# Computing the dt projection of a state-space block with its weights loaded and 512 tokens moved, in a fused three-block kernel

## The chip, the cores and the metric

The kernel is one program on one core of a Trainium2 chip. The metric is the device time of one execution in microseconds (us), the median of several runs. A core has a matrix engine (TensorE, PE in the profile, whose weight loads are listed as PEld), a vector engine (DVE), a scalar engine (ACT), GpSimd (POOL), and DMA queues driven from the SyncE (SP) and POOL instruction streams. Each engine works through its own stream in order; the streams meet at semaphores. A matmul here has a loaded operand (up to 128 columns that stay in the array) and a moved operand (up to 512 columns that stream through it); its result goes to PSUM.

## What is computed

The reference runs three blocks on x (2 sequences of 512 tokens, 1024 features): a Mamba-2 block with an MLP, a quantised product with a context, and a feed-forward block. The change lies in the first block. Cut to what matters:

```
h = rmsnorm(layernorm(x)) * ln1_w
z, xs, Bs, Cs, dt = split(h @ w_in.T)      # widths 1024, 256, 256, 1024, 8
xBC = silu(causal_conv4([xs, Bs, Cs]) + conv_b)
dt  = softplus(dt + dt_bias)               # 8 heads
a   = dt * -exp(A_log)                     # its cumulative sums per chunk of 128 tokens
...                                        # decays, attention within a chunk, states from chunk to chunk
y   = (Y + D * xs) * silu(z);  y @ w_out.T
```

The dt projection is thus a product of the 1024 tokens (2 x 512) with 1024 features by only 8 columns of weights.

## The kernel before

Activations are kept with features on the partitions: `AH` and `AL` are [128, 8, 1024], the high and low part of the normalised input (8 feature tiles, 1024 tokens). A product of single precision is made of three matmuls in the reduced form of fp32: high weights by high activations, high by low, low by high (`three`, line 656 holds the matmul). One block of 128 output features is `block_mm`: 8 feature tiles x 3 x 2 halves of 512 tokens = 48 matmuls with a 128x128 load each.

The work around the change, in the order in which TensorE takes it (block at line 651 and below):

- `first_pair(0)`: the first two convolution blocks, into the PSUM pairs `ps[0]` and `ps[1]`, as the activation tiles come in.
- The dt projection (lines 713 to 719): for each of 8 tiles of 128 tokens and each of 8 feature tiles, the activations are the loaded operand (128x128) and the weights are moved, 16 columns (high and low part of 8 heads, line 716) and then 8 columns (low activations by high weights, line 718). That makes 128 matmuls, whose result has tokens on the partitions, in `ps[2]`.
- `conv_pair(1)` to `conv_pair(5)`: two convolution blocks each, for `ps[0]` and for `ps[1]`. Each block waits for its weights (`s_ready`) and for VectorE to be done with the former block of this PSUM pair (`s_conv`). Between `conv_pair(4)` and `conv_pair(5)` stand two small matmuls for the cumulative sums (lines 726, 727).
- Then two waits, for `s_conv` at 14 (VectorE has finished all 12 convolution blocks) and for `s_csx` at 2, and the state-space stage: 8 chunks of 128 tokens. Each chunk begins with 12 matmuls of a z block into `ps[0]` (`block_mm(ps[0], ..., range(0, 2))`), then come two matmuls of the decay rows into `ps[1]` (line 741), two into `ps[2]` (line 748, which also waits until ScalarE has done all 12 silus), 6 more of z, the transposes (line 754), 6 more of z, line 759, the other 24 of z, and the head products (766, 767, 770).

VectorE follows with its own list. `conv_pair(i)` at line 1557: for each of the two blocks it makes the low part of the weights of a block two further on (`weights_lo`, line 1222, waits for ScalarE's high part), waits until TensorE has summed its block, and applies the four taps (line 1566 and three times line 1568); the last tap signals `s_conv`. Ahead of `conv_pair(0)` VectorE scales the residual input (line 1554, 8 instructions). After `conv_pair(0)` come the dt steps (lines 1579 to 1598): 14 small operations on 128x64 which go back and forth with ScalarE (an exponential, a logarithm, another exponential: lines 1146 to 1149). Then the loop of the other pairs.

ScalarE's list: `conv_silu` (line 1136) makes for each block the high part of the weights (line 920, when TensorE is done with the old weights of this slot), waits for the taps (`s_conv`) and applies silu (line 1141). `conv_silu(0, 0)` stands ahead of the dt functions, the loop of the others behind them.

Weights come by SyncE's queue, two raw slots; block n is loaded (line 389) when the low part of block n - 2 is made. GpSimd stores the scaled residual and copies x in DRAM after line 1554 (lines 594, 595, 4 MB each).

```
for t in range(NC):
    for k in range(KT):
        pe.matmul(ps[2][:, col:col + 2 * HEADS], AH[:, k, tok], wdt_hl[:, k, :, :], ...)
        ins = pe.matmul(ps[2][:, col:col + HEADS], AL[:, k, tok], wdt_hl[:, k, 0, :], ...)
```

Of the kernel before, what the change touches and what calls it, by code (L numbers as in the profile page):

```python
# [8 lines left out]
ACT = mybir.ActivationFunctionType  # L9

P = 128
BATCH, SEQ, DM = 2, 512, 1024
TOK = BATCH * SEQ
KT = DM // P
HEADS, GROUPS = 8, 2
HPG = HEADS // GROUPS
CHUNKS = SEQ // P
NC = BATCH * CHUNKS
TAPS = 4
CONV_TILES = (2 * 256 + DM) // P  # L20
# [124 lines left out]
def build(nc, x_t, ctx, w_mamba, w_dt, w_gu, w_dn, f_gu, f_dn, b_gu, b_dn, params, shapes_only,  # L145
# [9 lines left out]
    AH = at("act_hi", 0, [P, KT, TOK], F32R)  # L155
    AL = at("act_lo", 32 * KB, [P, KT, TOK], F32R)
# [13 lines left out]
    scr_r = at("scratch_r", R0, [P, 8, TOK], F32)  # L170
# [47 lines left out]
    def scr_u(j):  # L218
        return scr_r[:, j, :]

    def scr_c(j):
        return scr_c0[:, j, :] if j < 4 else scr_c1[:, j - 4, :]

# [46 lines left out]
    shp = small("tri_ident_mask", [P, 3, P])  # L270
# [5 lines left out]
    wdt_hl = small("w_dt_hi_lo", [P, KT, 2, HEADS], F32R)  # L276
# [23 lines left out]
    ps = [nc.alloc_psum_tensor(f"pair{i}", [P, TOK], F32) for i in range(4)]  # L300
# [6 lines left out]
    HALF = (slice(0, H), slice(H, TOK))  # L307
# [3 lines left out]
    def sem(name):  # L311
        return nc.alloc_semaphore(name)
# [11 lines left out]
    s_hs, s_hfree = sem("hs_ready"), sem("h_region_free")  # L324
    s_conv, s_silu = sem("conv_summed"), sem("conv_silu")
    s_dtm, s_dte, s_dts, s_csm, s_csx, s_exps = (sem(n) for n in ("dt_summed", "dt_exp_in", "dt_act", "cs_summed", "cs_exp_in", "cs_exp"))
    s_seq = sem("sequence_columns_ready")
    s_stage, s_bx, s_rr = sem("chunk_stage_free"), sem("bx_chunk_ready"), sem("cs_rhs_ready")
    s_yt, s_cs, s_ecs, s_msk, s_dec = sem("y_taken"), sem("cs_rows"), sem("exp_cs"), sem("cs_masked"), sem("decay_ready")
# [321 lines left out]
    def _(pe):  # L651
# [9 lines left out]
        def block_mm(out, wi, ks=range(KT), last_inc=s_used):  # L661

            for k in ks:
                ins = three(out, wi, k, AH[:, k, :], AL[:, k, :], k == 0, k == KT - 1)
            if last_inc is not None:
                ins.then_inc(last_inc, 1)
# [29 lines left out]
        for k in range(KT):  # L696
            pe.wait_ge(s_x[k], 16)
            ins = ones_mm(ps[2], hs[:, k, :], k == 0, k == KT - 1)
# [10 lines left out]
        pe.wait_ge(s_ready, 2)  # L709
        first_pair(0)  # L710

        for t in range(NC):
            col = t * 2 * HEADS
            tok = slice(t * P, (t + 1) * P)
            for k in range(KT):
                pe.matmul(ps[2][:, col:col + 2 * HEADS], AH[:, k, tok], wdt_hl[:, k, :, :],  # L716
                          start=k == 0, stop=False, skip_group_check=True)
                ins = pe.matmul(ps[2][:, col:col + HEADS], AL[:, k, tok], wdt_hl[:, k, 0, :],
                                start=False, stop=k == KT - 1, skip_group_check=True)
        ins.then_inc(s_dtm, 1)  # L720

        with pe.Fori(1, CONV_TILES // 2 - 1) as i:
            conv_pair(i)

        pe.wait_ge(s_csx, 1)
        pe.matmul(ps[2][:, 256:320], tri, a_all[:, :, :], start=True, stop=True)
        pe.matmul(ps[2][:, 320:384], ones[:, :], a_all[:, :, :], start=True, stop=True).then_inc(s_csm, 1)
        conv_pair(CONV_TILES // 2 - 1)
        pe.wait_ge(s_conv, CONV_TILES + 2)
        pe.wait_ge(s_csx, 2)  # L730


        with pe.Fori(0, BATCH) as b:
            for c in range(CHUNKS):
                q = b * CHUNKS + c
                pe.wait_ge(s_ready, q + (N_Z + 1))
                pe.wait_ge(s_z, q + 1)
                block_mm(ps[0], c % 2, range(0, 2), None)
                pe.wait_ge(s_rr, q + 1)
                for g in range(GROUPS):  # L740
                    ins = pe.matmul(ps[1][:, g * 512:(g + 1) * 512], ones[:, :], cs_rhs[:, g * HPG:(g + 1) * HPG, :],  # L741
                                    start=True, stop=False, skip_group_check=True)
                ins.then_inc(s_cs, 1)
                pe.wait_ge(s_bx, q + 1)
                pe.wait_ge(s_silu, CONV_TILES)
                pe.wait_ge(s_yt, q + 1)
                for g in range(GROUPS):
                    pe.matmul(ps[2][:, g * 512:(g + 1) * 512], bx_cur[:, 2 + g, :],  # L748
                              xbc[:, 4 + g * HPG:4 + (g + 1) * HPG, bass.ds(b * SEQ + c * P, P)],
                              start=True, stop=True)  # L750
                block_mm(ps[0], c % 2, range(2, 3), None)
                pe.wait_ge(s_state, b * (CHUNKS + 1) + (c + 1))
                for j in range(4):
                    ins = pe.transpose(ps[3][:, j * P:(j + 1) * P], bx_cur[:, j, :], ident)
                ins.then_inc(s_stage, 1)
                block_mm(ps[0], c % 2, range(3, 4), None)
                pe.wait_ge(s_ecs, q + 1)
                for g in range(GROUPS):
                    ins = pe.matmul(ps[1][:, g * 512:(g + 1) * 512], ident_bf[:, :],
                                    mask_bf[:, :].unsqueeze(1).to_broadcast([P, HPG, P]),  # L760
                                    start=False, stop=True, skip_group_check=True)
                ins.then_inc(s_msk, 1)
                block_mm(ps[0], c % 2, range(4, KT))
                pe.wait_ge(s_att, q + 1)
                for h in range(HEADS):
                    pe.matmul(ps[2][:, h * P:(h + 1) * P], x_dt[:, h, :], att[:, h, :], start=True, stop=False)  # L766
                    ins = pe.matmul(ps[2][:, h * P:(h + 1) * P], state[:, h, :], c_dec[:, h, :], start=False, stop=True)  # L767
                ins.then_inc(s_y, 1)
                for g in range(GROUPS):
                    ins = pe.matmul(ps[3][:, g * 512:(g + 1) * 512], b_tm[:, g, :], x_end[:, g * HPG:(g + 1) * HPG, :],  # L770
                                    start=True, stop=True)
                ins.then_inc(s_st, 1)
# [109 lines left out]
        for k in range(KT):  # L882
            pe.wait_ge(s_q1, k + 1)
            for half in range(2):
                ins = pe.matmul(ps[3][:, half * 512:(half + 1) * 512], ones_bf[:, :], q1[:, k, half * 512:(half + 1) * 512],
                                start=k == 0, stop=k == KT - 1)
            if k == KT - 1:
                ins.then_inc(s_row, 1)
            for o in range(2):
                ins = ctx_mm(o, k)  # L890
# [15 lines left out]
    def _(act):  # L906
# [229 lines left out]
        def conv_silu(i, j0):  # L1136
            for s in range(2):
                weights_hi_at(i, 2, j0 * 2 + s + 2, s)
                act.wait_ge(s_conv, i * 2 + (j0 * 2 + s + 3))
                tile = xbc[:, i * 2 + (j0 * 2 + s), :]  # L1140
                act.activation(tile, tile, ACT.Silu).then_inc(s_silu, 1)

        conv_silu(0, 0)

        act.wait_ge(s_dte, 1)
        act.activation(ncs_all[:, :, :], ncs_all[:, :, :], ACT.Exp).then_inc(s_dts, 1)
        act.wait_ge(s_dte, 2)
        act.activation(gtot_all[:, :, :], a_all[:, :, :], ACT.Ln).then_inc(s_dts, 1)
        act.activation(par[:, PA:PA + HEADS], par[:, PA:PA + HEADS], ACT.Exp).then_inc(s_dts, 1)
        with act.Fori(0, CONV_TILES // 2 - 2) as i:  # L1150
            conv_silu(i, 1)
        act.wait_ge(s_csx, 2)
        act.activation(gtot_all[:, :, :], gtot_all[:, :, :], ACT.Exp).then_inc(s_exps, 1)
        act.activation(dend_all[:, :, :], dend_all[:, :, :], ACT.Exp).then_inc(s_exps, 1)
# [61 lines left out]
    def _(dve):  # L1216
# [355 lines left out]
                ins.then_inc(s_conv, 1)  # L1572

        conv_pair(0)


        dtf = dt_all[:, :, :]
        dve.wait_ge(s_dtm, 1)
        dtp = ps[2][:, 0:NC * 2 * HEADS].rearrange("p (a two b) -> p a two b", a=NC, two=2)
        own.then(TT(dtf, dtp[:, :, 0, :], par[:, PDT:PDT + HEADS].unsqueeze(1).to_broadcast([P, NC, HEADS]), ALU.add))  # L1580
        own.then(TT(dtf, dtp[:, :, 1, :], dtf, ALU.add))
        own.then(STT(ncs_all[:, :, :], dtf, -1.0, dtf, ALU.mult, ALU.max))
# [15 lines left out]
        STT(a_all[:, :, :], dtf, -1.0, par[:, PA:PA + HEADS].unsqueeze(1).to_broadcast([P, NC, HEADS]),  # L1598
            ALU.mult, ALU.mult).then_inc(s_csx, 1)

        with dve.Fori(1, CONV_TILES // 2 - 1) as i:
            own.enter(i - 1, 7)
            conv_pair(i)
            own.leave(CONV_TILES // 2 - 2)


        dve.wait_ge(s_csm, 1)
# [195 lines left out]
```

## Time and profile before

| | us |
|---|---|
| median of 3 runs | 2303.24 (2302.9 to 2304.55) |
| the profiled execution, its own time | 2303.8 |
| its span, first to last instruction | 2302.0 |
| PE busy | 2153.9 (94%) |
| DVE busy | 1778.3 (77%) |
| ACT busy | 1007.7 (44%) |
| mean granted TensorE clock | 0.963 |

How to read it: the engines' busy times overlap each other; "idle before" in a row is the time in which the engine waited ahead of the instruction, with what released it; a granted clock of 1.00 is 2.4 GHz and 0.50 is 1.2 GHz. The durations of pipelined matmuls overlap as well, so what one costs is read from the distance between starts, or from the chain, where a stretch is divided by its count. The stretch that the change touches lies between 54 us and 240 us of the span.

### The profile page before, as it was taken

To read this page: it belongs to the slowest core of one execution; us is meant where nothing else is said; L and a number is where in the kernel's file an instruction comes from. 1 tells how busy PE (TensorE), PEld (TensorE's weight loads), DVE (VectorE), ACT (ScalarE), POOL (GpSimd) and SP (SyncE) were. 2 spreads that over 40 slices of the span, in tenths; PEclk is the share of its full clock that TensorE was granted. 3 is DMA by queue.
4 is the path that set the end of the run, shared out by engine and by line. 5 is a ranking of instruction groups with operands and counts; after the bars stand their busy time and mean duration, and the time that the engine had idled before them with its cause. 6 is when DMAs were issued, how large, how long until landed. Compare 5 with 4: busy or idle time off the path is not lost.

```text
span 2302.0 us, 26720 instructions
## 1 busy us (share of the span) xinstructions
PE 2153.9 (94%) x9346; PEld 1715.3 (75%) x9346; DVE 1778.3 (77%) x2518; ACT 1007.7 (44%) x1596; POOL 118.0 (5%) x195
## 2 busy tenths in 40 slices
PE   6998998978999999999999966689999999999999
PEld 2886776856888888888888822468888888788887
DVE  4755556469777888887978778889898888788785
ACT  3333223325555555554544331555545555444442
POOL 0000110000000000000000000000000000000000
PEclk8799999989999999999999978799999999999999
DMA  3411002524778888889330221156666666674301
GB/s 114 165 46 46 19 28 72 150 39 134 279 274 285 298 299 289 293 300 350 123 134 1 75 82 73 56 177 237 217 226 221 219 226 213 224 279 142 115 19 55
DMA packets 124316, 379.42 MB, mean 165 GB/s; under 512 B 14432, under 2 KB 14560, under 8 KB 120544
## 3 DMA queue, kind: packets, MB, share of 16 engines
q1 hardware_dynamic: 105456, 308.61, 39.1%
q0 software_dynamic: 18736, 69.22, 8.3%
q8 instruction: 70, 1.15, 0.2%
q14 instruction: 54, 0.44, 0.1%
HBM read 312.76 MB, written 69.21 MB: 166 GB/s over the span
## 4 chain that ended last, share of the span: by engine, by line
PE 84%; DVE 10%; DMA 2%; ACT 2%; issue 2%; DVEq 0%; SPq 0%; ACTq 0%
PE pair L823 40%; PE pair L848 23%; PE pair L656 14%; PE pair L684 3%; DVE ring_lo L1326 1%; DVE comb_lo L1376 1%; DMA wd_spill<-down_formed 1%; PE pair L767 1%; PE pair L766 1%; DMA down_formed<-f_dn 1%; PE pair L748 1%; PE pair L741 1%; DMA coeff_in<-b_dn 1%; PE pair L770 1%; PE pair L716 1%
## 5 line engine op out<-in xcount | busy, mean ns | idle before, releaser
L823 PE MATMUL pair<-comb_lo,ring_hi 128*128 128x512 f32 x1568 | 615.2, 392 | 0.0
L848 PE MATMUL pair<-inner_ring_a,ring_hi 128*128 128x512 f32 x1120 | 345.0, 389 | 0.6 <-DVE second_copy_b L1430 0.3
L823 PEld LDWEIGHTS pair<-comb_lo,ring_hi 128*128 128x128 f32 x1568 | 298.1, 190 | 61.2
L823 PE MATMUL pair<-comb_hi,ring_hi 128*128 128x512 f32 x672 | 265.7, 395 | 32.9 <-DVE comb_lo L1376 22.9
L823 PE MATMUL pair<-comb_hi,ring_lo 128*128 128x512 f32 x672 | 264.4, 393 | 0.0
L848 PEld LDWEIGHTS pair<-inner_ring_a,ring_hi 128*128 128x128 f32 x1120 | 210.1, 188 | 44.9 <-issue 1.4
L848 PE MATMUL pair<-inner_ring_a,ring_lo 128*128 128x512 f32 x560 | 217.8, 389 | 0.0
L823 PE MATMUL pair<-comb_hi_b,ring_hi 128*128 128x512 f32 x448 | 176.4, 394 | 15.0 <-ACT first_copy_b L1077 8.2
L823 PE MATMUL pair<-comb_hi_a,ring_hi 128*128 128x512 f32 x448 | 175.7, 392 | 10.8 <-ACT first_copy_a L1077 10.1
L823 PEld LDWEIGHTS pair<-comb_hi,ring_hi 128*128 128x128 f32 x672 | 128.0, 190 | 64.7 <-issue 26.9
L656 PE MATMUL pair<-act_hi,weights_hi 128*128 128x512 f32 x448 | 151.1, 419 | 26.6 <-DVE act_lo L1269 18.7
L823 PE MATMUL pair<-comb_hi_b,ring_lo 128*128 128x512 f32 x448 | 175.7, 392 | 0.0
L823 PE MATMUL pair<-comb_hi_a,ring_lo 128*128 128x512 f32 x448 | 175.0, 391 | 0.0
L998 ACT ACTIVATE ring_hi<-ring_sum 128x512 fp32r<-128x512 f32 x168 | 106.0, 631 | 143.3 <-DVE ring_sum L1313 138.9
L823 PEld LDWEIGHTS pair<-comb_hi,ring_lo 128*128 128x128 f32 x672 | 127.9, 190 | 27.1
L656 PE MATMUL pair<-act_lo,weights_hi 128*128 128x512 f32 x448 | 141.6, 398 | 0.0
L656 PE MATMUL pair<-act_hi,weights_lo 128*128 128x512 f32 x448 | 141.1, 397 | 0.0
L848 PE MATMUL pair<-inner_ring_b,ring_hi 128*128 128x512 f32 x448 | 138.1, 389 | 0.1
L656 PEld LDWEIGHTS pair<-act_hi,weights_hi 128*128 128x128 f32 x448 | 85.5, 194 | 52.7 <-issue 35.8
L848 PEld LDWEIGHTS pair<-inner_ring_a,ring_lo 128*128 128x128 f32 x560 | 105.1, 188 | 21.8
L1096 ACT ACTIVATE pair<-pair 128x1024 f32<-128x1024 f32 x84 | 84.7, 1009 | 72.7 <-DVE pair L1460 72.3
L1326 DVE TENSOR_TENSOR ring_lo<-ring_sum,ring_hi 128x512 fp32r<-128x512 f32 x168 | 115.0, 685 | 0.0
(343 smaller groups left out, 3931.9 us busy)
## 6 DMA issues: line engine op xcount, KB each, us to landing
coeff_in<-f_gu SPq DMA_DIRECT2D x56, 512.0 KB, 5.0
coeff_in<-b_gu SPq DMA_DIRECT2D x56, 512.0 KB, 5.9
base_in<-b_gu SPq DMA_DIRECT2D x56, 512.0 KB, 4.4
weights_raw<-w_mamba SPq DMA_DIRECT2D x28, 512.0 KB, 3.4
raw_a<-w_gu SPq DMA_DIRECT2D x28, 512.0 KB, 6.1
raw_a<-w_gu SPq DMA_DIRECT2D x56, 256.0 KB, 5.6
u_spill<-gate_a POOLq DMA_DIRECT2D x56, 256.0 KB, 5.4
coeff_in<-f_dn SPq DMA_DIRECT2D x28, 512.0 KB, 4.8
```

The costliest lines, as they stand in the source:

```text
L656: ins = pe.matmul(out[:, half * 512:(half + 1) * 512], w[:, wi, wcol * P:(wcol + 1) * P], a[:, half * 512:(half + 1) * 512], start=first a ...
L684: ins = pe.matmul(out[:, half * 512:(half + 1) * 512], ones[:, :], src[:, half * 512:(half + 1) * 512], start=first, stop=last)
L716: pe.matmul(ps[2][:, col:col + 2 * HEADS], AH[:, k, tok], wdt_hl[:, k, :, :], start=k == 0, stop=False, skip_group_check=True)
L741: ins = pe.matmul(ps[1][:, g * 512:(g + 1) * 512], ones[:, :], cs_rhs[:, g * HPG:(g + 1) * HPG, :], start=True, stop=False, skip_group_che ...
L748: pe.matmul(ps[2][:, g * 512:(g + 1) * 512], bx_cur[:, 2 + g, :], xbc[:, 4 + g * HPG:4 + (g + 1) * HPG, bass.ds(b * SEQ + c * P, P)], star ...
L766: pe.matmul(ps[2][:, h * P:(h + 1) * P], x_dt[:, h, :], att[:, h, :], start=True, stop=False)
L767: ins = pe.matmul(ps[2][:, h * P:(h + 1) * P], state[:, h, :], c_dec[:, h, :], start=False, stop=True)
L823: ins = pe.matmul(out, wt[:, slot, col], a, start=t in (0, 1, 3) and kk == 0 and n == 0, stop=kk == KH - 1 and n == 2, skip_group_check=True)
L848: ins = pe.matmul(out, wt[:, slot, col], a, start=t in (0, 1, 3) and k == 0 and n == 0, stop=k == SC_PAIRS - 1 and n == 2, skip_group_chec ...
L998: act.activation(WRH[:, slot, :], src, ACT.Copy).then_inc(s_whi, 1)
L1096: act.activation(dif_ps[:, :], dif_ps[:, :], ACT.Abs, accum_out=coef_all[:, kind, n:n + 1]).then_inc(s_ab, 1)
L1326: TT(WRL[:, slot, :], src, WRH[:, slot, :].bitcast(F32), ALU.subtract).then_inc(s_wlo, 1)
```

## The change

It has three parts. First, the dt projection: the weights (16 or 8 columns) become the loaded operand and 512 tokens are moved, 32 matmuls in place of 128. The result now has the heads on 16 partitions; ScalarE copies it to an SBUF tile of 16 x 1024, TensorE does `conv_pair(1)` meanwhile, and then eight full-fp32 matmuls with that tile as the loaded operand and a 16x16 identity moved turn it back to tokens on partitions, in `ps[3]`. Second, in order to fit, ScalarE takes the copy ahead of `conv_silu(0, 0)` and does `conv_silu(0, 1)` ahead of the dt functions, and VectorE does `conv_pair(1)` ahead of the dt steps. Third, TensorE enters the state-space stage with a wait for `s_conv` at 13 alone; the waits for 14 and for `s_csx` stand behind the first 12 matmuls of z.

```diff
+    dt_rows = scr_r[0:2 * HEADS, 0, :]
...
+    s_dtr, s_dtc = sem("dt_rows_summed"), sem("dt_rows_copied")
...
         first_pair(0)
+        for k in range(KT):
+            for half in HALF:
+                pe.matmul(ps[2][0:2 * HEADS, half], wdt_hl[:, k, :, :], AH[:, k, half],
+                          start=k == 0, stop=False, skip_group_check=True)
+                ins = pe.matmul(ps[2][0:HEADS, half], wdt_hl[:, k, 0, :], AL[:, k, half],
+                                start=False, stop=k == KT - 1, skip_group_check=True)
+        ins.then_inc(s_dtr, 1)
+        conv_pair(1)
+        pe.wait_ge(s_dtc, 1)
         for t in range(NC):
-            col = t * 2 * HEADS
-            tok = slice(t * P, (t + 1) * P)
-            for k in range(KT):
-                pe.matmul(ps[2][:, col:col + 2 * HEADS], AH[:, k, tok], wdt_hl[:, k, :, :],
-                          start=k == 0, stop=False, skip_group_check=True)
-                ins = pe.matmul(ps[2][:, col:col + HEADS], AL[:, k, tok], wdt_hl[:, k, 0, :],
-                                start=False, stop=k == KT - 1, skip_group_check=True)
+            ins = pe.matmul(ps[3][:, t * 2 * HEADS:(t + 1) * 2 * HEADS], dt_rows[:, t * P:(t + 1) * P],
+                            shp[0:2 * HEADS, 1, 0:2 * HEADS], start=True, stop=True)
         ins.then_inc(s_dtm, 1)
-        with pe.Fori(1, CONV_TILES // 2 - 1) as i:
+        with pe.Fori(2, CONV_TILES // 2 - 1) as i:
             conv_pair(i)
...
         conv_pair(CONV_TILES // 2 - 1)
-        pe.wait_ge(s_conv, CONV_TILES + 2)
-        pe.wait_ge(s_csx, 2)
+        pe.wait_ge(s_conv, CONV_TILES + 1)
...
                 block_mm(ps[0], c % 2, range(0, 2), None)
+                pe.wait_ge(s_conv, CONV_TILES + 2)
+                pe.wait_ge(s_csx, 2)
                 pe.wait_ge(s_rr, q + 1)
...
+        act.wait_ge(s_dtr, 1)
+        act.activation(dt_rows, ps[2][0:2 * HEADS, :], ACT.Copy).then_inc(s_dtc, 1)
         conv_silu(0, 0)
+        conv_silu(0, 1)
...
-        with act.Fori(0, CONV_TILES // 2 - 2) as i:
-            conv_silu(i, 1)
+        with act.Fori(0, CONV_TILES // 2 - 3) as i:
+            conv_silu(i, 2)
...
         conv_pair(0)
+        conv_pair(1)
...
-        dtp = ps[2][:, 0:NC * 2 * HEADS].rearrange("p (a two b) -> p a two b", a=NC, two=2)
+        dtp = ps[3][:, 0:NC * 2 * HEADS].rearrange("p (a two b) -> p a two b", a=NC, two=2)
...
-        with dve.Fori(1, CONV_TILES // 2 - 1) as i:
-            own.enter(i - 1, 7)
+        with dve.Fori(2, CONV_TILES // 2 - 1) as i:
+            own.enter(i - 2, 7)
             conv_pair(i)
-            own.leave(CONV_TILES // 2 - 2)
+            own.leave(CONV_TILES // 2 - 3)
```

## Rows read from the trace of the kernel before

**Rows 1.** Shares of the chain that ended last, whole span, by engine
```profile
PE 84%; DVE 10%; DMA 2%; ACT 2%; issue 2%; DVEq 0%; SPq 0%; ACTq 0%
```

**Rows 2.** Busy time in five stretches: PE, PEld, DVE, ACT, POOL, granted clock, DMA share, GB/s
```profile
54.35:78.63 24.28, 24.28 (x97) 19.85 (x97) 21.78 (x19) 12.11 (x11) 0.00 (x0) 0.90 0.00 1
78.63:101.49 22.86, 22.86 (x130) 22.86 (x128) 20.54 (x18) 2.00 (x2) 1.57 (x2) 0.60 0.65 241
101.49:213.60 112.11, 112.11 (x485) 92.39 (x485) 61.55 (x68) 37.96 (x37) 2.50 (x2) 0.97 0.23 78
213.60:221.68 8.08, 0.14 (x2) 0.01 (x1) 6.32 (x5) 1.35 (x2) 0.00 (x0) 0.68 0.21 65
221.68:226.84 5.16, 5.16 (x13) 4.11 (x13) 1.41 (x5) 2.05 (x2) 0.00 (x0) 0.51 0.00 0
```

**Rows 3.** The same columns, the dt stretch and what follows
```profile
78.63:83.30 4.67, 4.67 (x44) 4.67 (x42) 4.67 (x5) 0.00 (x0) 0.00 (x0) 1.00 0.00 0
83.30:101.49 18.19, 18.19 (x88) 18.19 (x87) 15.87 (x14) 2.00 (x2) 1.57 (x2) 0.50 0.82 303
101.49:107.20 5.71, 5.71 (x15) 4.45 (x16) 2.48 (x11) 5.57 (x7) 0.00 (x0) 0.50 1.05 391
```

**Rows 4.** Chain that ended last, in order of time: start us, us, what
```profile
191.66 0.22 PE pair L727 x2
191.88 21.87 PE pair L656 x96
...
220.08 1.29 DVE conv_out L1568
...
221.68 5.32 PE pair L656 x12
227.00 1.72 PE pair L741 x4
...
239.81 0.22 PE pair L767 x2
```

**Rows 5.** ScalarE in order of time: start us, us, what, [idle before]
```profile
74.81 1.06 ACT L920 ACTIVATE weights_hi<-weights_raw 128x1024 fp32r<-128x1024 f32 x1 [1.32 <-PE pair L656]
...
93.05 1.06 ACT L1141 ACTIVATE conv_out<-conv_out 128x1024 f32<-128x1024 f32 x1 [15.88 <-DVE conv_out L1568]
...
107.28 1.28 ACT L920 ACT_TABLE_LOAD   x1
```

**Rows 6.** VectorE in order of time, around the dt stretch
```profile
77.30 9.17 DVE L1554 TENSOR_TENSOR hs<-hs,scratch_r 128x1024 f32<-128x1024 f32 x8
...
86.59 1.23 DVE L1222 TENSOR_TENSOR weights_lo<-weights_raw,weights_hi 128x1024 fp32r<-128x1024 f32 x1
...
101.67 0.23 DVE L1580 TENSOR_TENSOR dt_all<-pair,params 128x64 f32<-128x64 f32 x1 [0.16 <-PE pair L718]
```

**Rows 7.** ScalarE's copy of a PSUM pair: least, median, most ns, first and last start
```profile
L1170 ACT ACTIVATE z_gate<-pair x8: 1024/1025/1025, 239.7 to 384.2; 128x1024 f32 x8
```

**Rows 8.** ScalarE, one later block from weights to silu
```profile
126.24 1.06 ACT L920 ACTIVATE weights_hi<-weights_raw 128x1024 fp32r<-128x1024 f32 x1 [0.54 <-PE pair L656]
...
134.21 1.06 ACT L1141 ACTIVATE conv_out<-conv_out  x1 [6.91 <-DVE conv_out L1568]
```

**Rows 9.** Time from issue to landing of the weight loads, and of the 4 MB store
```profile
DMA to landing us min/median/max: 3.2/3.4/18.9
...
hs_spill<-hs POOLq DMA_DIRECT2D x1, 4096.0 KB, 15.8
```

**Rows 10.** The entry of the state-space stage, ScalarE, VectorE and PE in order of time
```profile
210.58 1.06 ACT L1141 ACTIVATE conv_out<-conv_out 128x1024 f32<-128x1024 f32 x1 [5.26 <-DVE conv_out L1568]
...
221.39 1.06 ACT L1141 ACTIVATE conv_out<-conv_out 128x1024 f32<-128x1024 f32 x1 [6.49 <-DVE conv_out L1568]
...
204.12 1.23 DVE L1222 TENSOR_TENSOR weights_lo<-weights_raw,weights_hi 128x1024 fp32r<-128x1024 f32 x1 [4.14 <-ACT weights_hi L920]
...
221.68 1.22 PE L656 MATMUL pair<-act_hi,weights_hi 128*128 128x512 f32 x2 [7.94 <-DVE conv_out L1568]
```

## The prediction

> **What bounds the kernel now.** I read the chain that ended last first: TensorE holds 84% of it, VectorE 10% [rows 1], so time is won where TensorE does less or waits less. Then the busy time by stretches around the change [rows 2]: from 54.35 to 213.60 us TensorE is busy without a gap, then it does nothing for 8.08 us, then it goes on. In the dt stretch, 78.63 to 101.49, it is busy for all of 22.86 us, but the granted clock is 0.60 there. Cut in two [rows 3], the clock is 1.00 for 4.67 us and 0.50 (1.2 GHz) for 18.19 us, and it stays at 0.50 for the first 5.71 us of the convolution block behind it. So the 128 short matmuls cost twice: 42 of their loads take 4.67 us at full clock (0.11 us each), 87 take 18.19 us at half clock (0.21 us each), and the next block starts slow. The last reading is who else works in these stretches: VectorE scales the residual until 86.4 us and only then begins the taps of the first block [rows 6]. These rows are what the dt stretch hides today.
>
> **The dt projection itself.** A matmul that moves 512 columns costs 21.87 / 96 = 0.228 us at full clock, and 5.32 / 12 = 0.443 us at half clock [rows 4]. 32 of them are 7.3 us, so the projection ends at 78.63 + 7.3 = 85.9 us in place of 101.49. No row has a load of 16 columns; the nearest is the 128-column load of rows 4, which the 0.228 us includes, and I take that. Less than 512 columns at 2.4 GHz, 0.213 us and 6.8 us in all, it can't be. The upper bound of a matmul that moves 512 columns is that of full fp32, 1.72 us for the four records of two matmuls of line 741, 0.86 us each [rows 4], 27.5 us in all. The low end stands nearer, since the operands keep the reduced type that line 656 has.
>
> **What is late next.** The 15.6 us are not all won, since the next convolution block needs its PSUM pair and its weights. ScalarE made the high part of weight block 2 at 74.81 us [rows 5]. Now this instruction is queued behind the new copy, and that behind the end of the projection. Step by step: the projection ends at 85.9, 0.3 us for the semaphore (the last tap ended at 220.08 + 1.29 = 221.37, TensorE began at 221.68 [rows 4]), a copy of 1.03 us (a pair on 128 partitions [rows 7]; I take the same for 16 partitions with as many elements each, bounds 0.3 and 1.1 us), the high part 1.06 us, so VectorE gets it at 88.4. Before, VectorE began the low part at 86.59, and the taps were done when silu started, at 93.05: 6.46 us later [rows 5, 6]. From 88.4 that gives 94.8, and TensorE starts `conv_pair(1)` at 95.1 in place of 101.49. **Gain: 6.4 us.** TensorE stands still from 85.9 to 95.1, which is a new wait of 9.2 us, made of VectorE's work for the greater part; the queue order on ScalarE alone is 1.8 us of it.
>
> **The clock behind that gap.** After 8.08 us without work the clock is 0.51 for the next 5.16 us [rows 2]. The new gap is as long, so I take the same: 12 matmuls at 0.443 in place of 0.228 us, 2.6 us lost. This is no more than before, where the same block started slow as well, for 5.71 us [rows 3]. The term is zero, with bounds of 2.8 us gained (the clock holds) and 0.8 us lost (12 matmuls more or fewer by where the clock returns). The Trainium skill, "TensorE: Matmul & The Clock Gate", Part 1, says that the gate follows how busy TensorE has been and that idle gaps give the slow clock back. By that rule the projection of 32 matmuls would keep the clock, and the gap behind it would lose it, as I have it. But in rows 3 the engine is busy all the time and the clock falls nonetheless, so "busy" in the profile's sense is not enough, and a rival below comes from this.
>
> **Turning back.** Eight full-fp32 matmuls, two records each. Lines 727 (64 columns) and 767 (128 columns) both take 0.22 us for one such matmul [rows 4], so the moved columns don't set it and I take 8 x 0.22 = **1.8 us lost**, at half clock 3.5 us, and not under 0.9 us (one record each).
>
> **The moved lists.** VectorE now does the taps of `conv_pair(1)` ahead of the dt steps. Does the fourth pair of blocks wait? Call E the end of TensorE's `conv_pair(1)`. Before, that end was at 101.49 + 96 x 0.228 + 2.6 for the slow start = 126.0, and the high part of the next weights began at 126.24, 0.2 us later; from there to the silu of the block just summed there are 7.97 us [rows 8], so the taps end at E + 8.2. The dt steps with ScalarE's three functions and its table loads then hold both engines until 7.05 us after the taps (101.51, when the taps were over, to 108.56, the end of the last table load [rows 5, 6]), E + 15.2. Then come 7.97 us for the next block, E + 23.2, and 0.3 us for the semaphore: E + 23.5. TensorE wants this PSUM pair at E + 1.8 + 2 x 48 x 0.228 = E + 23.6. So the dt steps just fit. I cost them at nothing; every us that they are longer is one lost. The blocks after it need 8.2 us of VectorE against 10.9 us of TensorE and catch up. The dt steps were free before in the same way, under `conv_pair(1)`. On SyncE's queue nothing is moved, but its two loads of blocks 4 and 5 are issued 1.6 to 2 us later, in the traffic of the two 4 MB transfers; one load took 18.9 us to land there [rows 9]. Block 4 would be in at 108.5 at the latest; it is wanted then at the earliest, and at 113 at the latest. Free.
>
> **The two waits.** After the last block of the convolution TensorE waited 7.94 us for the taps [rows 10]. Now it does 12 matmuls of z first: their weights were made at 204.12 + 1.23 us, and `s_conv` at 13 was there when silu started at 210.58 [rows 10], ahead of 213.60. They take 2.7 us inside the gap; the decay rows then start when the taps are done, 221.7 less the shift, in place of 227.0. Of the 5.3 us between, 2.6 us are the slow clock, and 5.4 us of standing still remain, so I expect it to be slow again, now under lines 741 and 748. Silu is over 1.1 us after the taps, while line 741 takes 3.4 us at half clock, so it isn't late. **Gain: 12 x 0.228 = 2.7 us**, with bounds of 0 (ScalarE or VectorE late with the first chunk) and 5.3 us (the clock holds). In the other seven chunks these waits are met already.
>
> **Sum.** 6.4 - 1.8 + 2.7 = 7.3 us. The profiled execution took 2303.8 us, 1.8 us more than its span; 7.3 less is 2296.5. It lies 0.56 us over the median of the three runs, so the forecast is 2303.24 - 7.3 = 2295.9, 2296.0 rounded. Behind 240 us I expect every row to be as it was, earlier by this much.
>
> **Rivals.** (1) The clock falls in the new projection as well, because only 16 of 128 columns of the array have work. For it: the old stretch fell after 4.67 us although busy [rows 3]. Against: that one moved 16 columns per load, the new one 512. If it falls after 4.7 us, 11.4 matmuls cost 0.215 us more each, 2.5 us: 2298.4. Read strictly, the skill page's rule of the busy gate speaks against this rival. (2) The dt steps or the late loads don't fit, and TensorE waits for `s_conv` ahead of the fourth pair. The margin is 0.1 us; a chain 3 us longer gives 2299.0, within no change. (3) One of the gaps doesn't cost the clock: 2.6 us more are won, 2293.3. (4) Slower: a narrow load takes the matmul out of its fast form, and it costs as full fp32, 0.86 us. Then the projection ends at 106.1, the block starts at 115.3, 13.8 us late, plus 1.8, less 2.7: 2316. It decides from 0.46 us for one matmul on, (7.3 + 7.3) / 32. Against it: before, lines 716 and 718 are one record each with the same two tensors, where full fp32 shows two. (5) The change does nothing that shows: that would need the new gap to reach to 101 us, 6 us longer than VectorE's list allows.
>
> **How the numbers follow.** Forecast 0.63, with a range of its own of 2294 to 2298; (1) 0.12; (2) 0.10; (3) 0.08; (4) 0.04; the rest, (5) among it, 0.03. The range goes from under (3) to over (2): 2292.8 to 2299.8, and leaves out (4), (5) and part of each tail. A measurement can tell 0.2%, 4.6 us, so the border is 2298.6. Faster: all of the forecast and (3), two thirds of (1), 0.79. Same: (2), the rest of (1) and most of (5), 0.16. Slower: (4) and a little, 0.05.
>
> **What would show it.** In the profile after: line 656 idle some 9 us ahead of `conv_pair(1)`, released by line 1568; the projection 7 to 7.5 us long at clock 1.00; eight turning matmuls in about 1.8 us; no idle time of TensorE between there and the last block; about 5.4 us of idle time ahead of line 741. Wrong would be a projection over 10 us, a third idle stretch between 110 and 210 us, or a later stage whose length has changed by over 1 us.

## The result: 0.3% less time, and the profile after

The changed kernel takes 2294.73 us (median of 9 runs, 2293.19 to 2299.6) against 2302.9 us (9 runs, 2300.32 to 2305.02) for the kernel before: 0.9971 of the time, 95% interval 0.9962 to 0.9980, which is 4.6 to 8.8 us less. (The ratio is that of all runs on record; the two medians alone differ by 8.2 us, a ratio of 0.9965.) The forecast was 2296.0 us, 7.3 us less. The profiled execution took 2296.97 us, with a span of 2295.2 us.

In this execution TensorE reaches the projection 1.1 us later than in the one before (79.74 us in place of 78.63); 0.5 us of it is a longer wait for the input at the start (6.7 us in place of 6.2). So I compare lengths and not times. The busy time by stretches (us; PE, PEld, DVE, ACT, POOL; granted clock; DMA share; GB/s), to be laid beside [rows 2, 3]:

```profile
79.74:87.05 7.31, 7.31 (x33) 2.83 (x31) 7.31 (x7) 0.00 (x0) 0.00 (x0) 1.00 0.00 0
87.05:95.96 8.91, 0.24 (x2) 0.03 (x1) 6.85 (x7) 3.35 (x4) 1.57 (x2) 0.74 0.74 263
95.96:101.70 5.74, 5.74 (x14) 4.50 (x15) 3.76 (x3) 1.89 (x2) 0.00 (x0) 0.51 1.04 385
95.96:210.75 114.79, 114.45 (x501) 94.26 (x502) 69.25 (x72) 37.05 (x37) 2.50 (x2) 0.98 0.29 103
210.75:213.50 2.75, 2.75 (x13) 2.05 (x11) 1.42 (x2) 1.06 (x1) 0.00 (x0) 1.00 0.00 0
213.50:218.56 5.06, 0.11 (x1) 0.00 (x0) 4.90 (x4) 0.02 (x1) 0.00 (x0) 0.91 0.33 104
218.56:225.20 6.64, 6.64 (x9) 2.88 (x10) 2.64 (x6) 3.35 (x3) 0.00 (x0) 0.55 0.00 0
```

The projection takes 7.3 us at full clock. Then TensorE stands still for 8.9 us, and the next blocks begin at half clock for 5.7 us. At the entry of the state-space stage the 12 matmuls of z run at full clock, 5.1 us of standing still remain, and the half clock has moved under the decay rows and line 757 (748 before). The waits of TensorE from 50 to 240 us, in total, times and longest, say the same:

```profile
PE pair L659 <- DVE conv_out L1580: 9.0, 2, 8.7
PE pair L750 <- DVE conv_out L1580: 5.0, 1, 5.0
```

ScalarE and VectorE inside the new gap (the copy, the high part, the low part with its 1.81 us of waiting, and the first tap), beside [rows 5, 6], and then TensorE's first matmuls behind the gap:

```profile
87.32 1.01 ACT L1153 ACTIVATE scratch_r<-pair 16x1024 f32<-16x1024 f32 x1 [12.81 <-PE pair L720]
88.24 1.04 ACT L929 ACTIVATE weights_hi<-weights_raw 128x1024 fp32r<-128x1024 f32 x1
...
87.42 0.17 DVE L1571 COPY conv_par<-params 128x10 f32<-128x10 f32 x1
89.39 1.22 DVE L1234 TENSOR_TENSOR weights_lo<-weights_raw,weights_hi 128x1024 fp32r<-128x1024 f32 x1 [1.81 <-ACT weights_hi L929]
90.53 1.34 DVE L1578 TENSOR_SCALAR conv_out<-pair,conv_par 128x1024 f32<-128x1024 f32 x1
...
95.96 1.19 PE L659 MATMUL pair<-act_hi,weights_hi 128*128 128x512 f32 x2 [8.68 <-DVE conv_out L1580]
```

**One length for the whole change.** From the first matmul of the projection to the start of the last state update everything that the change touches is inside. Before, that is 391.7 - 78.6 = 313.1 us, after it 386.4 - 79.7 = 306.7 us, 6.4 us less; a second profile of the changed kernel has 383.4 - 76.7 = 306.7 again. The last state updates, in the view of this line (durations in ns; first and last start), before, changed, and changed again:

```profile
L1647 DVE SCALAR_TENSOR_TENSOR state<-state,sequence_columns,pair x64: 340/342/344, 245.4 to 391.7; 128x128 f32<-128x128 f32 x64
```
```profile
L1660 DVE SCALAR_TENSOR_TENSOR state<-state,sequence_columns,pair x64: 339/340/343, 240.1 to 386.4; 128x128 f32<-128x128 f32 x64
```
```profile
L1660 DVE SCALAR_TENSOR_TENSOR state<-state,sequence_columns,pair x64: 339/342/343, 237.0 to 383.4; 128x128 f32<-128x128 f32 x64
```

The whole time scatters by 4 to 6 us from run to run; this length repeats within 0.1 us where the clock changes at the same places. Where the clock rises earlier or later behind a gap, it moves by up to some 1.4 us, as the run with GpSimd later shows below. It is the sharper measure, and is called "the stretch".

### The profile page after: what moved, and what is told of

Its sections match the earlier page's. It is cut to its first block, busy times and chain, and to the rows that moved or that the text cites. A ratio compares the mean times of both kernels' runs of the same rounds, so it can differ in the third digit from the quotient of the medians.

```text
span 2295.2 us, 26531 instructions
## 1 busy us (share of the span) xinstructions
PE 2141.0 (93%) x9263; PEld 1695.7 (74%) x9266; DVE 1779.3 (78%) x2518; ACT 1005.7 (44%) x1595; POOL 118.4 (5%) x195
## 4 chain that ended last, share of the span: by engine, by line
PE 82%; DVE 11%; DMA 2%; ACT 2%; issue 1%; SPq 1%; DVEq 0%; ACTq 0%
PE pair L832 41%; PE pair L857 22%; PE pair L659 12%; PE pair L687 3%; DVE ring_lo L1338 1%; DVE comb_lo L1388 1%; DMA wd_spill<-down_formed 1%; PE pair L750 1%; DVE conv_out L1580 1%; PE pair L757 1%; PE pair L776 1%; PE pair L775 1%; DMA down_formed<-f_dn 1%; PE pair L779 1%; SPq L446 1%
## 5 line engine op out<-in xcount | busy, mean ns | idle before, releaser
L832 PE MATMUL pair<-comb_hi,ring_hi 128*128 128x512 f32 x672 | 266.2, 396 | 32.6 <-DVE comb_lo L1388 22.9
```

The source lines that it names most:

```text
L832: ins = pe.matmul(out, wt[:, slot, col], a, start=t in (0, 1, 3) and kk == 0 and n == 0, stop=kk == KH - 1 and n == 2, skip_group_check=True)
```

## The experiments

| kernel | median, us | of the time before (95% interval) | the stretch, us |
|---|---|---|---|
| before | 2302.9 | | 313.1 |
| changed | 2294.7 | 0.9971 (0.9962 to 0.9980) | 306.7 |
| projection alone | 2299.9 | 0.9983 (0.9974 to 0.9992) | 309.3 |
| two waits alone | 2300.6 | 0.9985 (0.9976 to 0.9994) | 310.3 |
| changed, copy behind | 2293.1 | 0.9956 (0.9943 to 0.9969) | 303.8 |
| changed, fillers in both gaps | 2293.1 | 0.9960 (0.9946 to 0.9974) | 301.1 |
| changed, filler in the first gap | 2293.1 | 0.9963 (0.9949 to 0.9976) | 303.7 |
| changed, filler in the second gap | 2294.2 | 0.9966 (0.9952 to 0.9980) | 303.7 |
| changed, GpSimd later | 2293.9 | 0.9961 (0.9948 to 0.9975) | 304.7 |
| before, scaling later | 2303.5 | 1.0002 (0.9992 to 1.0011) | 313.1 |
| changed, once more | 2294.8 | 0.9970 (0.9959 to 0.9980) | 306.7 |
| changed, scaling later | 2287.5 | 0.9928 (0.9915 to 0.9942) | 296.2 |
| changed, scaling later, GpSimd later, more z ahead | 2280.8 | 0.9902 (0.9887 to 0.9917) | 290.7 |

The kernel before was measured again beside the experiments; its medians there are 2302.2 to 2303.3 us, and each ratio is against those. The stretch comes from one profile of each kernel.

### The two halves of the change, each alone

The projection with its moved lists, and the waits of the kernel before:

```diff
-        pe.wait_ge(s_conv, CONV_TILES + 1)
+        pe.wait_ge(s_conv, CONV_TILES + 2)
+        pe.wait_ge(s_csx, 2)
...
                 block_mm(ps[0], c % 2, range(0, 2), None)
-                pe.wait_ge(s_conv, CONV_TILES + 2)
-                pe.wait_ge(s_csx, 2)
```

> Only the new dt projection with its moved lists; the two waits stand ahead of the state-space stage as before. My theory (three separate terms): from the start of the projection to the start of the second pair of blocks 16.2 us in place of 22.9, then 2.0 us of turning back and 0.6 us of waiting ahead of the fourth pair, so 4.0 us less than before, about 2299; the gap ahead of the state-space stage is 8 us again. Rival (the two edits only pay together): less than 1.5 us are won.

The reverse, the waits moved and the old projection kept:

```diff
-        pe.wait_ge(s_conv, CONV_TILES + 2)
-        pe.wait_ge(s_csx, 2)
+        pe.wait_ge(s_conv, CONV_TILES + 1)
...
                 block_mm(ps[0], c % 2, range(0, 2), None)
+                pe.wait_ge(s_conv, CONV_TILES + 2)
+                pe.wait_ge(s_csx, 2)
```

> Only the two waits are moved behind the first 12 matmuls of z; the old dt projection stays. My theory: the gap falls from 7.9 to 5.0 us, and the slow clock moves from the 12 matmuls to lines 741 and 748, which take 6.5 us in place of 3.4; the end of line 748 comes 2.4 us earlier, about 2300.7. Rival (the wait that is left gives it all back, since the taps end the stage): the end of line 748 doesn't move, 0 us.

The stretch is 3.8 us shorter with the projection alone and 2.8 us with the waits alone, 6.6 us in sum, against 6.4 us for both. The halves add up, and the rival that they pay only together falls. With the projection alone the wait ahead of the state-space stage is 7.94 us, as before. With the waits alone the chain that ended last has the new order of the entry (start, us, what):

```profile
221.29 3.78 PE pair L742 x4
225.07 2.49 PE pair L749 x4
227.57 1.39 PE pair L656 x6
```

Line 742 (741 before) starts 5.7 us earlier than in [rows 4], and it takes 3.78 us in place of 1.72, line 749 takes 2.49. Half of what the earlier start gives goes to the clock (2.8 of 5.7 us), and the rival that the remaining wait gives all of it back is wrong as well.

### What the new gap is made of

ScalarE makes the high part of weight block 2 first, and takes the dt copy behind it:

```diff
-        act.wait_ge(s_dtr, 1)
-        act.activation(dt_rows, ps[2][0:2 * HEADS, :], ACT.Copy).then_inc(s_dtc, 1)
...
                 weights_hi_at(i, 2, j0 * 2 + s + 2, s)
+                if first and s == 0:
+                    act.wait_ge(s_dtr, 1)
+                    act.activation(dt_rows, ps[2][0:2 * HEADS, :], ACT.Copy).then_inc(s_dtc, 1)
```

> The changed kernel, but ScalarE takes the high part of weight block 2 first and the dt copy after it. My theory: 1.8 us of the new gap of 8.7 us are ScalarE's queue order, the rest is VectorE's scaling and taps; the gap is 6.9 us, the time 1.8 us under the changed kernel. Rival (the gap is ScalarE's alone): the gap falls by the copy and the high part and more, to under 3 us. Rival (VectorE sets it all): the gap stays at 8.7 us.

The gap is 6.86 us in place of 8.68:

```profile
91.65 1.19 PE L659 MATMUL pair<-act_hi,weights_hi 128*128 128x512 f32 x2 [6.86 <-DVE conv_out L1581]
```

That is the 1.8 us that the theory gives to ScalarE's queue order; both rivals are out. The stretch is 2.9 us shorter, 1.1 us more than the gap. The blocks behind it took 24.0 us in place of 24.7, and line 757 took 2.44 us in place of 2.85: both are a shorter time at half clock, and together they are this 1.1 us. The edit doesn't aim at them.

The rest of the gap should be VectorE's scaling and taps. So the scaling (9.2 us) moves behind the taps of the first pair, and the copy behind the high part of block 3:

```diff
         rsqrt(1, scr_u, 1.0 / DM, EPS)
-        for k in range(KT):
-            TT(hs[:, k, :], hs[:, k, :], scr_u(5), ALU.mult).then_inc(s_hs, 1)
...
         conv_pair(0)
+        for k in range(KT):
+            TT(hs[:, k, :], hs[:, k, :], scr_u(5), ALU.mult).then_inc(s_hs, 1)
         conv_pair(1)
```

> The changed kernel; VectorE scales the residual (8 instructions, 9.2 us) behind the taps of the first pair of blocks in place of ahead of them, and ScalarE takes the dt copy behind the high part of weight block 3. My theory (what is left of the first gap is VectorE's list): the taps of the first block are done at about 85 us, before the projection ends, the gap is under 0.5 us, the clock stays at 1.00 there, the stretch from the start of the projection to the end of the stage's last state update is 294 to 296 us (changed kernel 306.7), and the time is about 2284. Rival (the work is only moved): a gap of 3 us or more comes up ahead of the third or fourth pair, and the stretch is 300 us or more.

The gap is gone. The last matmul of the projection and the first of the second pair follow each other at the normal distance:

```profile
86.85 0.39 PE L720 MATMUL pair<-act_lo,w_dt_hi_lo 128*8 128x512 f32 x1
87.08 0.62 PE L659 MATMUL pair<-act_hi,weights_hi 128*128 128x512 f32 x2
```

The stretch is 296.2 us (375.9 - 79.7), 10.5 us under the changed kernel, and no other wait came up ahead of the third or fourth pair:

```profile
L1661 DVE SCALAR_TENSOR_TENSOR state<-state,sequence_columns,pair x64: 339/340/343, 229.6 to 375.9; 128x128 f32<-128x128 f32 x64
```

The time is 2287.5 us, 3.5 us over what I had expected, though 7.2 us under the changed kernel. In the profiles 2.0 us of the difference lie behind the stretch (1910.8 us there against 1908.8).

The control is the same move with the old projection:

```diff
         conv_pair(0)
+        for k in range(KT):
+            TT(hs[:, k, :], hs[:, k, :], scr_u(5), ALU.mult).then_inc(s_hs, 1)
...
         dve.wait_ge(s_dtm, 1)
```

> The kernel before, old dt projection, with VectorE's scaling moved behind the taps of the first pair. My theory: the 22.9 us of the old projection hide VectorE's list either way, so the stretch from the projection to the last state update stays at 313.1 us (within 1 us) and the time at 2303. Rival (VectorE's scaling held this kernel too): the time falls by 2 us or more.

The stretch is 313.1 us (392.1 - 79.0), unchanged, and the time 1.0002 of the kernel before (0.9992 to 1.0011):

```profile
L1646 DVE SCALAR_TENSOR_TENSOR state<-state,sequence_columns,pair x64: 339/340/343, 245.7 to 392.1; 128x128 f32<-128x128 f32 x64
```

So VectorE's scaling costs nothing under the long projection and sets the start of the next block under the short one. This is the pair of runs that shows what the old 22.9 us had covered.

### The clock in the two gaps

36 matmuls that move 512 columns against 16 loaded ones fill the first gap, 20 the second. Their results are used nowhere; they are work added to what the reference needs.

```diff
+        def filler(n):
+            for i in range(n):
+                pe.matmul(ps[3][0:2 * HEADS, HALF[i % 2]], wdt_hl[:, 0, :, :], AH[:, 0, HALF[i % 2]], start=True, stop=True)
...
         ins.then_inc(s_dtr, 1)
+        pe.wait_ge(s_t, 2)
+        filler(36)
         conv_pair(1)
...
         pe.wait_ge(s_conv, CONV_TILES + 1)
+        filler(20)
```

> The changed kernel with 36 matmuls of 512 moved columns and 16 loaded ones in the first gap and 20 in the second, results not used. They compute nothing that is needed; they fit in the gaps (8.2 of 8.7 us, 4.6 of 5.0 us). My theory: the granted clock is 1.00 through both gaps, the second pair of blocks takes 21.9 us in place of 24.7, lines 750 and 757 take 3.4 us in place of 6.6, and the time is 6 us under the changed kernel. Rival (narrow loads don't hold the clock): the clock falls in the gaps nonetheless and the time is that of the changed kernel or up to 1 us more.

With both fillers, the projection with its gap, and then the second pair of blocks (columns as above):

```profile
78.79:94.86 16.07, 15.71 (x69) 6.18 (x67) 14.17 (x13) 3.36 (x4) 1.57 (x2) 1.00 0.40 141
94.86:116.88 22.02, 22.02 (x97) 17.99 (x97) 12.82 (x11) 5.07 (x5) 0.00 (x0) 1.00 0.96 350
```

The clock stays at 1.00 and the pair takes 22.0 us in place of 24.7. The rival that narrow loads don't hold the clock is wrong: 68 such matmuls in 16 us held it. The stretch is 5.6 us shorter, as expected (6). But the time is only 1.6 us under that of the changed kernel. Two more kernels fill one gap each, and the changed kernel runs beside them. From the kernel with both fillers, first without the one in the second gap:

```diff
-        filler(20)
```

> The changed kernel with the 36 fillers of the first gap alone, results not used. Both theories have the stretch from the projection to the last state update 2.7 us shorter than the changed kernel, since the second pair of blocks starts at 2.4 GHz. Theory A (the later stages don't know of it, the spread of the medians hid it in the run with both fillers): the time falls by 2 to 3 us against the changed kernel of this call. Theory B (a clock held here is paid back later): the time is that of the changed kernel, within 1 us, and the stretch behind the last state update is 2 us longer.

Then without the one in the first gap:

```diff
-        pe.wait_ge(s_t, 2)
-        filler(36)
```

> The changed kernel with the 20 fillers of the second gap alone, results not used. The stretch from the projection to the last state update is 2.9 us shorter than the changed kernel's 306.7 us (lines 750 and 757 at 2.4 GHz). Theory A: the time falls by 2 to 3 us. Theory B: within 1 us of the changed kernel.

The third is without an edit.

> The changed kernel itself once more, on the same chip as the two filler runs, as what they are compared with. Expected 2294.7 us, its median before, within 1.5 us. If turning back costs the clock when it falls badly in time, as in the runs with the scaling moved, a profile of it may show 0.50 for some 3 us behind line 726; in the first profile it didn't.

The changed kernel repeats: 2294.78 us, and 306.7 us for the stretch. Each filler shortens the stretch by 3.0 us, and both together 5.6 us. The times fall by 1.7 us (first) and 0.6 us (second) against it. Behind the stretch, from the last state update to the end of the span, the profiles have 1909.4 us for the changed kernel here (2292.8 - 383.4), 1910.4 with the first filler, 1912.9 with the second and 1912.6 with both; the first profile of the changed kernel has 1908.8, the kernel before 1910.3. So the part of the kernel that nobody touched varies by 4 us over these profiles. Theory A, that the gain arrives whole, isn't borne out, and theory B, that it is paid back whole, isn't either: five or six runs, which scatter by 2.2 to 8 us, don't settle it.

The traces say how far the gain arrives. From the last state update to the first matmul of line 848 (857, 863, 862 and 864 in the other kernels), a part of the kernel that comes much later, it is 663.2 us before, 662.9 and 662.7 in the two profiles of the changed kernel, 662.8 with the first filler, 662.7 with the second and 663.1 with both. So no more than 0.4 us of it has been paid back by then, and all but 0.5 us of the variation lies behind that point. The two profiles with the second filler have the longest rests of all 13 profiles (the others have 1908.3 to 1911.7 us). Whether that comes from the filler or from chance stays open.

One place where the untouched part varies is seen. Before, TensorE waits 4.3 us for a copy of line 1084 near 2010 us, and its clock drops once behind it; in the first profile of the changed kernel the same wait is 3.5 us and the clock holds (the end of the wait and what follows before, and what follows in the changed kernel):

```profile
2010.00:2016.00 6.00, 4.67 (x14) 3.75 (x15) 4.00 (x6) 5.23 (x10) 0.54 (x1) 0.72 1.05 387
```
```profile
2006.00:2012.00 6.00, 6.00 (x28) 4.94 (x27) 3.27 (x5) 4.17 (x9) 0.16 (x1) 1.00 1.05 396
```

The length of the wait doesn't decide it: in the second profile of the changed kernel it is 3.4 us, and the clock falls behind it nonetheless. It holds there in one other profile, that with the copy behind, which also has the shortest rest behind the stretch (1908.3 us).

### GpSimd, and everything together

Ahead of the fourth pair the changed kernel has a short wait of 0.34 us, for VectorE's taps. Ahead of these taps stands a low part of weights that takes 2.75 us, where the others take 1.23, and GpSimd is at work in just this time:

```profile
144.85 0.70 PE L659 MATMUL pair<-act_hi,weights_hi 128*128 128x512 f32 x2 [0.34 <-DVE conv_out L1580]
...
121.83 1.23 DVE L1234 TENSOR_TENSOR weights_lo<-weights_raw,weights_hi 128x1024 fp32r<-128x1024 f32 x1 [4.38 <-ACT weights_hi L929]
136.41 2.75 DVE L1234 TENSOR_TENSOR weights_lo<-weights_raw,weights_hi 128x1024 fp32r<-128x1024 f32 x1 [1.03 <-ACT weights_hi L929]
...
135.53 0.61 POOL L605 COPY bx_chunk<-conv_out 128x512 f32 x1 [46.14 <-DVE a_all L1611]
136.19 1.89 POOL L606 TENSOR_TENSOR cs_rhs<-tri_ident_mask,a_all 128x1024 f32<-128x1024 f32 x1
```

So GpSimd waits for two more silus:

```diff
-        pool.wait_ge(s_silu, 4)
+        pool.wait_ge(s_silu, 6)
```

> The changed kernel; GpSimd's first copy and product of the state-space stage wait for 6 silus in place of 4. My theory (GpSimd's two instructions at 135.5 to 138.1 us made VectorE's low part take 2.75 us in place of 1.23, and this made TensorE wait ahead of the fourth pair): the low part there takes 1.23 us, TensorE doesn't wait there, the stretch from the projection to the last state update is 0.5 us shorter than 306.7. Rival (the dt steps alone are too long): the wait of 0.34 us stays.

The low part is back at 1.23 us and the wait is gone:

```profile
135.45 1.23 DVE L1234 TENSOR_TENSOR weights_lo<-weights_raw,weights_hi 128x1024 fp32r<-128x1024 f32 x1 [1.03 <-ACT weights_hi L929]
```

GpSimd's product now meets a later low part, and that one is slow in its turn (no wait of TensorE comes of it):

```profile
156.02 1.68 DVE L1234 TENSOR_TENSOR weights_lo<-weights_raw,weights_hi 128x1024 fp32r<-128x1024 f32 x1 [3.28 <-ACT weights_hi L929]
...
154.72 1.89 POOL L606 TENSOR_TENSOR cs_rhs<-tri_ident_mask,a_all 128x1024 f32<-128x1024 f32 x1
```

That GpSimd's work makes the low part slow, and this the wait, is shown. The stretch is 2.0 us shorter, of which some 0.5 us are this wait (the row behind the wait starts 0.95 us after the one before it, where 0.45 us is usual); most of the rest is a shorter time at half clock at the entry of the state-space stage (lines 750 and 757 take 5.2 us in the chain there, against 6.6 us), which this edit doesn't aim at.

Last, the moved scaling with the copy behind the high part of block 3, the later GpSimd, and 24 matmuls of z ahead of the taps in the first chunk of each sequence:

```diff
-                block_mm(ps[0], c % 2, range(0, 2), None)
+                block_mm(ps[0], c % 2, range(0, 4 if c == 0 else 2), None)
...
-                block_mm(ps[0], c % 2, range(2, 3), None)
+                if c:
+                    block_mm(ps[0], c % 2, range(2, 3), None)
...
-                block_mm(ps[0], c % 2, range(3, 4), None)
+                if c:
+                    block_mm(ps[0], c % 2, range(3, 4), None)
```

> The kernel of the run with the scaling moved, GpSimd waiting for 6 silus, and in the first chunk of each sequence 24 matmuls of z ahead of the wait for the taps in place of 12. My theory: the second gap falls from 5.0 to 2.3 us and the clock doesn't fall under lines 741 and 748 (their changed line numbers), so 4 to 6 us less than the run with the scaling moved alone, about 2279. Rival (the z matmuls were needed later in the chunk as cover): what the gap gives is lost again inside the first chunk, 0 to 1 us.

The second gap is 2.23 us, the decay rows run at full clock, and one short wait of 0.2 us comes up later in the chunk:

```profile
204.84 1.98 PE L750 MATMUL pair<-cs_rhs,ones 128*128 128x512 f32 x4 [2.23 <-DVE conv_out L1581]
```

The stretch is 290.7 us, 5.5 us under the run with the scaling moved, and the time is 2280.8 us, 0.9902 of the kernel before (0.9887 to 0.9917). This is the fastest version here. The half clock behind the second gap is gone with a gap of 2.23 us; behind gaps of 5.0 us it was there in every profile.

## Why the prediction was right, step by step

- **The projection** was to end after 7.3 us at full clock, and ended after 7.31. Rival 1 (the clock falls because 16 of 128 columns have work) didn't happen, in any profile, and the fillers held the clock in the gaps as well. The narrow result isn't what lets the clock fall. Before, it fell while TensorE moved 16 or 8 columns for each load of 128 columns [rows 3]; no run here tells the few moved columns from the dense loads. By the rule of the Trainium skill, "TensorE: Matmul & The Clock Gate", Part 1, that the gate follows how busy TensorE has been, the clock holds in the new projection, and this trace agrees (1.00 for 7.31 us); the old one, busy all the time and at 0.50 after 4.67 us, doesn't fit it as long as busy is what the profile calls busy.
- **The new gap** was put at 9.2 us and measured 8.9 (8.68 in the view of the waits): copy 1.01 us (1.03 taken), high part 1.04 (1.06), VectorE's list as before. Its split, 1.8 us for ScalarE's order and the rest for VectorE, is shown by the copy placed behind and the scaling moved.
- **From the projection's start to the second pair:** 16.22 us in place of 22.86, 6.6 us won (6.4 forecast).
- **The clock behind the gap:** 5.7 us slow before and after, so the term of zero was right, in its size too.
- **Turning back** took 1.9 us from its first matmul to the next block (1.8 taken). A load of 16 rows by 128 columns takes 0.187 us there, as one of 128 by 128 does (0.188); the 128 by 16 loads of the projection take 0.095. The 16 loads in the view of this line:

```profile
L726 PEld LDWEIGHTS pair<-tri_ident_mask,scratch_r x16: 181/187/187, 120.6 to 122.2; 16*128 16x128 f32 x16
```

- **The dt steps** were costed at nothing with 0.1 us to spare; 0.34 us of waiting was measured. The one step that failed is the assumption that VectorE's operations keep their durations when they move: with the dt steps 27 us later, the low part behind them fell together with GpSimd's two instructions, one of which waits for the last of these steps, and took 1.52 us longer. I had looked at every queue but GpSimd's. A second error went the other way. Without GpSimd's work there is no wait at all, and 1.52 us more make one of 0.34 to 0.5; so by estimate the chain had about 1 us to spare and not 0.1. That the wait stayed so small is luck.
- **The two waits** were to give 2.7 us, with 5.4 us of gap left and the slow clock moved; alone they gave 2.8 us in the stretch, with 5.0 us left.
- **The sum** was 7.3 us; the stretch gives 6.4: 6.6 won up to the second pair, 2.7 lost from there to the end of the convolution (114.79 us against 112.11 [rows 2]; 1.8 forecast, the rest is the fourth pair and the clock), and 2.4 won from there to the end of line 757 (14.45 us against 16.84; 2.7 forecast). The medians differ by 8.2 us, 1.8 more than the stretch; the interval of the ratio includes both. The forecast lies between the two, and nothing in its terms accounts for this 1.8 us, which is less than what the untouched part varies by: that the median came within 1.3 us of 2296.0 is in part luck.
- **Its own signs of being wrong.** A third idle stretch between 110 and 210 us is there, of 0.34 us. Another sign, a later stage whose length has changed by over 1 us, was seen: from the last state update to the end of the span it is 1910.3 us before and 1908.8 in the first profile of the changed kernel. The second profile has 1909.4, and kernels that differ from them only ahead of this part have 1908.3 to 1912.9. So "every row as it was" was too strict for this part, and the sign can't tell an effect of the change from this variation.

## What to carry to other kernels

A stage that is made shorter uncovers what the others did meanwhile: list, for each engine, the first instruction that now has to be done, and what is queued ahead of it. Here the matrix work fell by 15.6 us and 6.6 us arrived, until 9 us of vector work that nobody waited for was moved behind the work that TensorE needed; with the old projection the same move gave nothing. And a gap of 5 us or more cost its length plus the slow clock behind it here, so work that is independent of the wait belongs in the gap, as the matmuls of z show.

## What the runs showed of the hardware that I had not expected

- A VectorE operation with two SBUF inputs (128x1024, 1.23 us) took 2.75 us while GpSimd ran a product. It ended 1.08 us after GpSimd had (139.16 against 138.08 us). With GpSimd later the low part that it met took 1.68 us and ended 1.09 us after (157.70 against 156.61), and in the last kernel 1.49 us and 1.08 (144.88 against 143.80). However long they overlapped, the end followed GpSimd's by the same time, so VectorE seems to have done next to nothing until then. The Trainium skill, "SBUF — State Buffer", says in its table of terms that the shared pair of ports is held for a full instruction and the loser blocks; these rows agree.
- Behind turning back, eight short matmuls in 1.9 us between blocks that run densely, the clock can fall though TensorE never stood still. It held in eight profiles, the two of the changed kernel among them, but in the two kernels with the scaling moved it fell just behind, for 3.4 us (with the scaling moved, turning back, and then the slow time):

```profile
108.80:110.80 2.00, 2.00 (x17) 1.86 (x16) 0.31 (x1) 1.66 (x2) 0.00 (x0) 1.00 1.03 424
112.10:115.50 3.40, 3.40 (x11) 2.64 (x10) 3.33 (x4) 0.00 (x0) 0.00 (x0) 0.55 1.03 423
```

  That is 1.7 us lost. These two are also the only ones in which the DMA engines are busy all through turning back (share 1.03 and 1.02, against 0.08 and less in the other eight), with the two 4 MB transfers that come later there. Whether the short matmuls, the transfers or both let the clock fall, no run here separates.
- A copy from PSUM of 16 partitions by 1024 elements takes ScalarE 1.01 us, nearly as long as one of 128 partitions, 1.025 us [rows 7].
